# Context rows packed into full tiles, a stacked mixer output projection, and a new order of work in each slot

## What is computed

```python
x = layernorm(x + mixer(x))                    # input projection to 512, 4-tap causal convolution, silu,
                                               # xp projection, a scan with 16 states, out_w projection
x = layernorm(x + xattn(ctx_1024, x, ...))     # 8 heads of 128; keys and values from layernorm(ctx)
                                               # (77 rows) and from layernorm(x) (256 rows); Wq, Wkv, Wo
x = layernorm(x + moe(x, ...))                 # 8 experts, top 2, capacity 512, gather and scatter-add
```

## Time and profile before

| | |
|---|---|
| median of 3 runs | 1146.37 us (1145.55 to 1146.81) |
| profiled execution: its own time, its span | 1145.72 us, 1144.0 us |
| busy share of the span, PE / weight loads / DVE / ACT / POOL | 91% / 83% / 71% / 58% / 44% |
| mean granted TensorE clock | 0.966 of 2.4 GHz |

### The profile page before, as it was taken

The page is one execution under the profiler, slowest core; times in us unless marked ns, Lnnn a source line. Parts: engine busy times, 40 slices in busy tenths (PEclk is TensorE's granted clock), DMA queues, the critical chain, the costliest instruction groups (busy, mean ns, idle before and its releaser), DMA issues. The chain is left out here.

```text
span 1144.0 us, 23278 instructions
## 1 busy us (share of the span) xinstructions
PE 1039.8 (91%) x7026; PEld 954.4 (83%) x7026; DVE 815.3 (71%) x2068; ACT 663.3 (58%) x1689; POOL 508.5 (44%) x828
## 2 busy tenths in 40 slices
PE   5699999999999999999999999999999989479970
PEld 4589999898989898989898988999889989369960
DVE  4677878787878777777778777878687876346435
ACT  4465656565656565657566665566656656135535
POOL 1324263635354444445444545363636363425553
PEclk8899999999999999999999999999999999779995
DMA  9300000000000010010101010101010000375548
GB/s 302 114 13 11 22 29 23 32 23 24 27 24 30 10 36 17 20 32 20 32 22 32 19 32 23 31 20 32 22 31 20 11 19 11 148 240 85 78 50 295
DMA packets 37543, 59.01 MB, mean 52 GB/s; under 512 B 3890, under 2 KB 28308, under 8 KB 37396
## 3 DMA queue, kind: packets, MB, share of 16 engines
q1 hardware_dynamic: 29716, 44.51, 11.8%
q0 software_dynamic: 7680, 12.72, 5.4%
HBM read 31.33 MB, written 25.89 MB: 50 GB/s over the span
## 5 line engine op out<-in xcount | busy, mean ns | idle before, releaser
L1318 POOL TENSOR_SCALAR prob<-prob,rinv 128x333 f32<-128x333 f32 x256 | 141.3, 563 | 366.2 <-DVE rinv L1166 364.8
L469 PE MATMUL ps<-kv_lo,w_hi 128*128 128x256 f32 (+1 forms) x512 | 169.9, 332 | 2.8 <-DVE kv_lo L901 2.7
L823 ACT ACTIVATE prob<-ps,nmx 128x333 f32<-128x333 f32 x256 | 135.2, 536 | 37.2 <-DVE nmx L1158 37.0
L471 PE MATMUL ps<-kv_hi,w_hi 128*128 128x256 f32 (+1 forms) x512 | 153.6, 300 | 0.0
L470 PE MATMUL ps<-kv_hi,w_lo 128*128 128x256 f32 (+1 forms) x512 | 153.6, 300 | 0.0
L818 ACT ACTIVATE oT_hi<-ps 128x256 fp32r<-128x256 f32 x128 | 49.1, 383 | 176.3 <-PE ps L471 174.6
L901 DVE TENSOR_TENSOR pT_lo<-ps,pT_hi 128x512 fp32r<-128x512 f32 (+1 forms) x256 | 131.1, 550 | 2.1 <-ACT pT_hi L835 1.3
L496 PE MATMUL ps<-ident,prob 128*128 128x128 f32 (+1 forms) x768 | 126.6, 273 | 3.2 <-POOL prob L1318 2.3
L1158 DVE TENSOR_REDUCE nmx<-ps 128x2 f32<-128x666 f32 x128 | 108.3, 846 | 22.6 <-PE ps L471 22.0
L469 PE MATMUL ps<-pT_lo,v_hi 128*128 128x256 f32 (+1 forms) x384 | 108.6, 283 | 2.1 <-DVE pT_lo L901 1.1
L471 PE MATMUL ps<-pT_hi,v_hi 128*128 128x256 f32 (+1 forms) x384 | 108.3, 282 | 0.0
(11 more groups left out here) (207 smaller groups left out, 3057.8 us busy)
## 6 DMA issues: line engine op xcount, KB each, us to landing
wraw<-in_W SPq DMA_DIRECT2D x14, 512.0 KB, 6.2
slots<-initr SPq DMA_DIRECT2D x8, 520.0 KB, 11.0
xts<-in_xT SPq DMA_DIRECT2D x16, 256.0 KB, 2.7
xs<-in_x SPq DMA_DIRECT2D x16, 256.0 KB, 2.8
accd<-xrow SPq DMA_DIRECT2D x16, 256.0 KB, 2.2
xsl<-slots SPq DMA_DIRECT2D x7, 520.0 KB, 3.7
fx<-accd SPq DMA_DIRECT2D x6, 512.0 KB, 6.5
out<-fx SPq DMA_DIRECT2D x6, 512.0 KB, 4.0
```

What stands on the lines that cost most here:

```text
L469: pe.matmul(dst, hi1, lo2, start=first, stop=False, skip_group_check=True)
L471: return pe.matmul(dst, hi1, hi2, start=False, stop=last, skip_group_check=True)
L823: act.activation(prob[:, h % 2, t, 0:KEYS], ps[:, S0 + t, 0:KEYS], ACT.Exp, bias=nmx[:, h % 2, t:t + 1], accum_out=rsum[:, h % 2, t:t + 1] ...
L1318: pool.tensor_scalar(prob[:, h % 2, t, 0:KEYS], prob[:, h % 2, t, 0:KEYS], rinv[:, h % 2, t:t + 1], 1.0, ALU.mult, ALU.mult).then_inc(norm ...
```

## The change

Four things change.

First, the 16 x 77 context rows are read as ten tiles of 128 rows ("ctx" and "more" in the table, `cT` for the transposes, `vc` for two value units per tile). A tile's normalised transposed rows (`cx_hi`, `cx_lo`) and its values (`vst_hi`, `vst_lo`) are stored to DRAM (`keep_context`, `keep_values`) and each batch loads its 77 rows from there. The v units per batch go from six to four, `ctxT` goes. Tiles 0 and 1 are made in body -1, tile 2 in body 0, the others in every second body.

Second, the state and `out_w` are stacked into 96-row fp32r operands (`ys_x`, `oww_x`), so that `op` is two fp32r matmuls. SP loads `out_w` three times for it, and ACT copies the scanned state twice in front of its work of slot 4. The two operands of `cum` become fp32r too.

Third, the order: `in` is done two batches ahead ("aft"), with a body -2 in front; the loop covers batches 1 to 12; `xp` moves to slot 3, `op` to slot 4 and `ln` to slot 5; DVE and POOL steps move with them; one product of the scan's input (`ut`) goes from DVE to ACT.

Fourth, in each slot `weighted` comes ahead of `scores`, `turn` does all three blocks in one group directly behind `scores`, ACT drains the transposes ahead of the exponentials, and DVE writes `oT_lo` ahead of the maximum.

```diff
 UNITS = [
-    [("k", 1, "att"), ("in", 0, "nxt"), ("q", 1, "att"), ("v", 1, "att")],
-    [("k", 2, "att"), ("v", 2, "att"), ("in", 1, "nxt")],
-    [("k", 3, "att"), ("v", 3, "att"), ("q", 2, "att")],
-    [("k", 4, "att"), ("v", 4, "att"), ("ctxT", 0, "nxt")],
-    [("k", 5, "att"), ("q", 3, "att"), ("xp", 0, "nxt"), ("x2T", 0, "prv")],
-    [("k", 6, "att"), ("v", 5, "att"), ("op", 0, "nxt"), ("dots", 0, "prv")],
-    [("k", 7, "att"), ("ln", 0, "nxt")],
+    [("k", 1, "att"), ("q", 1, "att"), ("v", 1, "att")],
+    [("k", 2, "att"), ("v", 2, "att")],
+    [("k", 3, "att"), ("q", 2, "att")],
+    [("k", 4, "att"), ("v", 3, "att"), ("xp", 0, "nxt"), ("x2T", 0, "prv"), ("cT", 0, "ctx")],
+    [("k", 5, "att"), ("q", 3, "att"), ("op", 0, "nxt"), ("in", 0, "aft")],
+    [("k", 6, "att"), ("dots", 0, "prv"), ("vc", 0, "ctx"), ("cT", 0, "more"), ("ln", 0, "nxt")],
+    [("k", 7, "att"), ("in", 1, "aft"), ("vc", 1, "ctx"), ("vc", 0, "more"), ("vc", 1, "more")],
     [("k", 0, "nxt"), ("cum", 0, "prv"), ("q", 0, "nxt"), ("v", 0, "nxt")],
 ]
...
         def bodies(eng, body):
-            nxt, prv, att = {"nxt"}, {"prv"}, {"att"}
-            body(-1, 1, nxt, set())
-            body(0, 0, att | nxt, nxt)
-            with eng.Fori(0, (B - 2) // 2) as i:
-                for u in range(2):
-                    body(2 * i + 1 + u, (1 + u) % 2, att | nxt | prv, att | nxt if u == 0 else att | nxt | prv)
-            body(B - 1, (B - 1) % 2, att | prv, att | nxt | prv)
-            body(B, B % 2, prv, att | prv)
+            mid, back, had = {"att", "aft", "nxt", "prv"}, {"att", "prv"}, {"aft", "nxt"}
+            body(-2, 0, {"aft"}, set(), 0)
+            body(-1, 1, {"aft", "nxt", "ctx", "more"}, {"aft"}, 0)
+            body(0, 0, {"att", "aft", "nxt", "ctx"}, had, 2)
+            with eng.Fori(0, (B - 4) // 2) as i:
+                body(2 * i + 1, 1, mid | {"ctx"}, had, i + 3)
+                body(2 * i + 2, 0, mid, had, i + 3)
+            body(B - 3, 1, mid | {"ctx"}, had, CT - 1)
+            body(B - 2, 0, mid - {"aft"}, had, CT - 1)
+            body(B - 1, 1, back, {"nxt"}, CT - 1)
+            body(B, 0, {"prv"}, back, CT - 1)
...
-        SPLIT_AT = [[], [], [], [], [0, 1, 2], [3, 4], [5], [6, 7]]
+        HI_AT = [[], [0, 1], [2, 3, 4], [], [5], [], [], [6, 7]]
+        LO_AT = [[], [], [0, 1, 2], [], [3, 4], [5], [], [6, 7]]
...
+            sp.wait_ge(owx_set, 1)
+            for row in (0, 32, 64):
+                sp.dma_start(oww[row:row + NST + 1, :], out_w).then_inc(oww_ld, 16)
...
+            def keep_context(c):
+                need(sp, cxl_set, c + 1)
+                need_apart(sp, cx_st, 32 * c)
+                for d, part in zip(cx_tiles, (cx_hi, cx_lo)):
+                    sp.dma_start(d[bass.ds(c, 1)].rearrange("o p k t -> (o p) k t"), ap(part[:])).then_inc(cx_st, 16)
+            def keep_values(c):
+                need(sp, vcl_set, 2 * c + 2)
+                need_apart(sp, vc_st, 32 * c)
+                for d, part in zip(vc_tiles, (vst_hi, vst_lo)):
+                    sp.dma_start(d[bass.ds(c, 1)].rearrange("o p n -> (o p) n"), ap(part[:])).then_inc(vc_st, 16)
...
+                if "ctx" in have:
+                    next_context(tile + 1)
+                    keep_context(tile)
+                if "nxt" in have:
+                    need_apart(sp, cx_st, 32 * tile + 32)
+                    need_apart(sp, k_mm, 8 * b)
+                    for d, part in zip(cx_rows, (kv_hi[1 - par], kv_lo[1 - par])):
+                        sp.dma_start(ap(part[:, :, S:KEYS]), d[bass.ds(a, 1)].rearrange("o p k t -> (o p) k t")
+                                     ).then_inc(kvc_ld, 16)
+                if "ctx" in have:
+                    keep_values(tile)
+                if "nxt" in have:
+                    need_apart(sp, vc_st, 32 * tile + 32)
+                    need_apart(sp, av_mm, 8 * b + 4)
+                    if at(b, -1):
+                        sp.wait_ge(w_lo_set, 6)
+                    values(a, 0)
...
-            def turn(m, ring, tiles):
+            def turn(m, ring):
                 need(pe, norm_set, 2 * m + 2)
-                for j in tiles:
+                for j in range(KT):
...
-                    need(pe, ys_set, bb + 1)
+                        pe.wait_ge(owx_set, 5)
+                    need(pe, ysh_set, 2 * bb + 2)
+                    need(pe, ysl_set, bb + 1)
                     for t in range(NT):
-                        last = pe.matmul(g[:, t * D:(t + 1) * D], ys[:, t * P:(t + 1) * P], oww[:], start=True, stop=True)
+                        last = pe.matmul(g[:, t * D:(t + 1) * D], ys_x[:, t * P:(t + 1) * P], oww_x[:],
+                                         start=True, stop=True)
                     last.then_inc(op_mm, 1)
...
+                if name == "vc":
+                    need(pe, cxl_set, bb + 1)
+                    for k in range(KD):
+                        last = three(g[:], cx_hi[:, k, :], cx_lo[:, k, :], wpart(w_hi, 2, k, idx * 512, 512),
+                                     wpart(w_lo, 2, k, idx * 512, 512), k == 0, k == KD - 1)
+                    last.then_inc(vc_mm, 1)
...
+                    if prev2:
+                        hh = (h - 2) % H
+                        bb = b if h > 1 else b - 1
+                        weighted(m - 1, hh, bb)
                     if here:
                         scores(b, h)
-                    if prev2:
-                        hh = (h - 2) % H
-                        bb = b if h > 1 else b - 1
-                        weighted(m - 1, hh, 6 * bb + (3 if hh < 4 else 6))
                     if prev:
-                        turn(m, (h - 1) % 2, (0, 1))
-                    for i, (name, idx, who, place) in enumerate(units(h, have) + [(None,) * 4]):
-                        if i == min(TURN_AT[h], len(units(h, have))):
-                            if at(b, 0) and h == 1:
-                                pe.wait_ge(cvec_set, 1)
-                            if prev:
-                                turn(m, (h - 1) % 2, (2,))
-                        if name is None:
-                            break
-                        if free := before(place, b, have, had):
+                        if at(b, 0) and h == 1:
+                            pe.wait_ge(cvec_set, 1)
+                        turn(m, (h - 1) % 2)
+                    for name, idx, who, place in units(h, have):
+                        if free := before(place, b, tile, have, had):
                             need(pe, *free)
...
+                    act.activation(ut[:], g[32:32 + NST, 0:S], IDN, bias=v16[:, 1:2], scale=0.5).then_inc(ut_set, 1)
...
+                if name == "vc":
+                    need(act, vc_mm, 2 * bb + idx + 1)
+                    need(act, vc_st, 32 * bb)
+                    act.activation(vst_hi[:, idx * 512:(idx + 1) * 512], g, ACT.Copy).then_inc(vch_set, 1)
...
+                    if h == 4 and "nxt" in have:
+                        need(act, ys_set, b + 2)
+                        need(act, op_mm, b + 1)
+                        for row in (0, 64):
+                            act.activation(ys_x[row:row + NST, :], ys[:], ACT.Copy).then_inc(ysh_set, 1)
                     if prev2:
                         need(act, av_mm, n - 1)
                         need(act, wo_mm, n - 3)
                         act.activation(oT_hi[:, h % 2, :], ps[:, AVB, 0:S], ACT.Copy).then_inc(oTh_set, 1)
+                    if prev:
+                        need(act, av_mm, n - 1)
+                        need(act, t_mm, 2 * n - 1)
+                        act.activation(pT_hi[:, 0:2, :].rearrange("p j s -> p (j s)"), ps[:, T0, :],
+                                       ACT.Copy).then_inc(pTh_set, 1)
+                        need(act, t_mm, 2 * n)
+                        act.activation(pT_hi[0:CTX, 2, :], ps[0:CTX, T0 + 1, 0:S], ACT.Copy).then_inc(pTh_set, 1)
...
-            dve.memset(ys[:], 1.0)
+            dve.memset(oww[:], 0.0).then_inc(owx_set, 1)
+            dve.memset(ap(ys_x[:]), 0.0).then_inc(owx_set, 1)
...
+            dve.wait_ge(owx_set, 2)
+            dve.wait_ge(oww_ld, 48)
+            dve.memset(ap(ys_x[0:32, :]), 1.0)
+            dve.memset(ap(ys_x[64:96, :]), 1.0).then_inc(owx_set, 1)
+            dve.tensor_copy(oww_x[:], oww[:]).then_inc(owx_set, 1)
+            dve.wait_ge(owx_set, 4)
+            minus(oww_x[64:96, :], oww[64:96, :], oww_x[64:96, :]).then_inc(owx_set, 1)
...
+            def state_lo(b, par, *tile):
+                need(dve, ysh_set, 2 * b + 3)
+                minus(ys_x[32:32 + NST, :], ys[:], ys_x[0:NST, :]).then_inc(ysl_set, 1)
...
             STEPS_AT = {
...
-                (4, "C"): [("nxt", context_hi)],
-                (6, "A"): [("nxt", latents), ("prv", last_counts), ("prv", first_weight),
-                           ("prv", last_places)],
-                (6, "D"): [("nxt", latents_hi)],
-                (7, "D"): [("prv", last_slots)],
```

(51 more changed lines are left out.)

436 lines of the change are left out of this document (230 added, 206 removed).

## The result

The changed kernel takes 1180.91 us (median of 4 runs, 1180.07 to 1182.2) against 1146.59 for the kernel before on the same chip: a ratio of 1.030, 95% interval 1.0282 to 1.0318. It is slower, where 1131 was forecast.

The account below looks back on a forecast made before the run. PE's instruction count was taken to bound the loop. Work off PE -33.5, one turn less -1.4, ln -6, scan wait +15 and prologue +11.5 sum to -14.4 from 1145.7: 1131 us, range 1114 to 1143.

Parts of the forecast that it names:

- Work that leaves PE: PE's matmuls: fewer for v, op and cum, more for vc, in sum -33.5 us.
- `ln` now stands at the end of slot 5 ... late by some 0.4 us in even bodies and not in odd ones: Slot 5: ln, moved behind dots, waits less than before, a gain of 0.4 us on average, 15 bodies: -6 us.
- Theory A of e7: Behind ln in even passes: the clock falls because PE idles after dots; filling that hole gives 1170 us.
- The scan gets a new wait: Slot 4: block 2's transposes wait 1.0 us for the scan, state copies and oT copies; 15 bodies: +15 us.
- Late drain of `oT`: Rival, chance 0.12: oT's copies come late for block 2's transposes in every slot, up to 1152 us in its example.
- one turn less: Loop's back edge: the loop runs six times and not seven, -1.4 us.
- The prologue: Before the loop: first scores at 65 us, 20.5 us later, 9.0 of it moved work, so net cost 11.5 us.
- the gate: Prologue: DVE waits for three oww loads before its first tap, near 21 us; xp near 33, 13.5 us later.

Follow-up runs that it names:

- e8: Changed kernel with later oww wait, state copies behind oT_hi and ln ahead of vc, plus each vc unit computed twice: 1176.59 us, ratio 1.0238.
- e9: Changed kernel with later oww wait, state copies behind oT_hi and ln ahead of vc, plus op in plain fp32: 1154.47 us, ratio 1.0051.
- e2: Changed kernel with the transposes of block 2 behind the first unit of every slot again: 1190.54 us, ratio 1.0394.
- e4: Changed kernel with ln right behind dots, ahead of vc and cT: 1162.44 us, ratio 1.0139.
- e7: Changed kernel with ten useless PE matmuls of 256 columns between dots and ln in passes without vc: 1170.84 us, ratio 1.0214.
- e3: Changed kernel with ACT's two copies of the state behind oT_hi instead of ahead of it: 1159.37 us, ratio 1.0106.
- e11: e10 with the transposes of block 2 behind the first unit in slot 0 alone: 1137.04 us, ratio 0.9927.
- e10: Changed kernel with later oww wait, state copies behind oT_hi and ln ahead of vc, plus tile 1's vc last in the first pass: 1143.01 us, ratio 0.9947.
- e1: Changed kernel with DVE's wait for the three oww loads moved from ahead of the first tap to ahead of the state's low part: 1171.7 us, ratio 1.0219.

## Why the prediction was wrong

**"Work that leaves PE"** held. A unit of six costs 1.35 us on average and 1.57 in the loop (e8) where I had 1.39, and PE's counts fell as said. `op` saves about 0.68 us (1.06 to the next start before, 0.36 to 0.41 after), not 0.82, and less if the unit behind it is taken in: `op` and `in` together take 2.03 us in the changed kernel (460.38 to 462.41) and 2.40 with `op` in fp32 (e9, 449.14 to 451.54). So this term was too large by 2 to 7 us in all. That the saving is kept whole depends on what stands behind it, as e9 shows. Merging `turn`, costed at nothing, is a gain of about 10 us against a split in every slot (e2).

**"`ln` now stands at the end of slot 5 ... late by some 0.4 us in even bodies and not in odd ones"** is the step that failed. I followed `ln`'s input through DVE's order and left out its other condition, the bank that `dots` fills just ahead of it and DVE frees last. In place of 0.4 the even pass waits 1.70 (e4 removes 1.3 of it by another bank).

**The clock** is in no step, and that is the second failure. Each hole was priced at its own length. Shown: with the hole at `ln` filled by useless work (e7) or shortened (e4), the clock stays up in the whole loop; with the holes of slot 4 gone (e3) it stays up in four turns of six. The price is 1.4 to 1.5 us in a turn, some 10 us in all. Theory A of e7 is right in that taking idle time away keeps the clock up, but no single hole decides: e3 kept the hole of 1.72 us and lost the fall from the third turn on, and in e2 the clock fell behind four holes of 2.75 us and stayed up behind two more (716.71, 836.21). What makes it fall in one turn and not in the next is not settled by these runs.

**"The scan gets a new wait"** was right, too small: 1.21 and 1.44 us instead of 1.0 each. With the clock that it drags down it cost 21.5 us (e3) where I had +15.

**Late drain of `oT`**, my rival on the slower side: not in every slot. It shows in slot 0 and slot 4 only, and in slot 0 of the odd pass it is DVE's own return from the loop's back edge (1.90 us late, 1.18 of it on PE). Before, the back edge showed on PE itself, as 1.25; I had it in the sum as one turn less, and a wait of this size is still there in each turn. A unit in front hides most of it (1.18 to 0.28, e11).

**"The prologue"**: the gate was as said (first tap 23.12 for 21, xp 34.05 for 33). First scores are 6.9 us later than the 65 I gave. I took +7 for two `in` units, four `vc` units and the wait for the store together; it was 37.8 - 25.0 = 12.8. The store of tile 0 alone held ACT for 6.77 us, on the path: taking it off gave 6.8 (e10). The gate, which I had priced at its full length, is worth only 4.9 (e1), since xts and the store wait behind it.

**The sum of the loss.** Of the 39.4 us between first and last scores, 31 lie in the seven turns (118.9 on average against 114.5); a turn of 119.6 has 1.6 more than forecast at `ln`, 1.5 from the clock, 0.65 in slot 4 and 0.5 in slot 0 and at `v`. Another 0.8 of it, in which `op`'s smaller saving has a part, and the 8 us outside the seven turns, I have not placed; a wait of 2.75 us for `k_lo` in the first pass is among them. The last 3.4 us are `x2T` of the last batch, 8.21 for 4.33, behind POOL's scatters, which come 1.4 us later and take 2.5 longer. I did not follow them, and no run tested that.

## What to carry to other kernels

When a unit moves in a list that deals out banks in turn, work out for each place not only when its input is ready but who fills the bank three places ahead and who frees it: here that was worth 18.5 us (e4). An estimate that prices each hole at its length is too low when PE is nearly full, as holes of 1 to 2 us can also lower the clock behind them; look at the granted clock in windows of two microseconds before and after such a change. And price a change in the loop and in the prologue apart: here 1143 and 1137 us were reached with the same work as 1181, by order alone.
